# Rotary q of the attention: halves exchanged by row transfers from a copy, sine product on GpSimd, every pair of heads begun three pairs ahead

## The reference, cut to what matters

```
def _rotate_half(x):
    x1, x2 = jnp.split(x, 2, axis=-1)
    return jnp.concatenate([-x2, x1], axis=-1)

def _apply_rope(x, cos, sin):
    return x * cos + _rotate_half(x) * sin
...
q = (x @ Wq).reshape(Bd, Sd, H, DH + D_ROPE)
q_nope, q_rope = (q[..., :DH], q[..., DH:])
c_kv = x @ Wdkv
kv = (c_kv @ Wukv).reshape(Bd, Sd, H, 2 * DH)
k_rope = x @ Wkr
q_rope = _apply_rope(q_rope, cos, sin)
k_rope = _apply_rope(k_rope, cos, sin)
scores = q_nope . k_nope + q_rope . k_rope, scaled and causal
attn = jax.nn.softmax(scores, axis=-1)
```

## Time and profile before

| | us |
|---|---|
| runs of the kernel, median of 3 | 1650.55 |
| the profiled execution | 1647.6 |
| its span (first to last instruction) | 1645.7 |
| attention: first matmul of the stage, last heads | 39.63 to about 443 |

### The profile page before, as it was taken

The page is one execution under the profiler, slowest core; times in us unless marked ns, Lnnn a source line. Parts: engine busy times, 40 slices in busy tenths (PEclk is TensorE's granted clock), DMA queues, the critical chain, the costliest instruction groups (busy, mean ns, idle before and its releaser), DMA issues. The chain is left out here.

```text
span 1645.7 us, 38779 instructions
## 1 busy us (share of the span) xinstructions
PE 1309.8 (80%) x13740; PEld 1003.8 (61%) x13741; DVE 1047.7 (64%) x2173; ACT 611.3 (37%) x1322; POOL 626.1 (38%) x556
## 2 busy tenths in 40 slices
PE   2798999988547999994356878988889539999992
PEld 1355666666436998993223446666667428989981
DVE  6488888978773555554685666666565464555554
ACT  2366676666423333331255721111111213333330
POOL 0254554455203333321003346666666212333320
PEclk9899999999758999997578959999999759999996
DMA  4556566564357111113100000000000257111115
GB/s 139 138 153 175 153 161 188 160 158 145 113 181 303 47 46 51 48 36 121 51 0 13 0 14 2 3 2 3 2 3 2 78 177 287 48 51 45 47 36 166
DMA packets 98815, 145.94 MB, mean 89 GB/s; under 512 B 32961, under 2 KB 76738, under 8 KB 96386
## 3 DMA queue, kind: packets, MB, share of 16 engines
q1 hardware_dynamic: 87746, 118.00, 24.0%
q0 software_dynamic: 8832, 24.13, 4.9%
q10 hardware_dynamic: 2112, 2.10, 0.4%
HBM read 87.57 MB, written 39.32 MB: 77 GB/s over the span
## 5 line engine op out<-in xcount | busy, mean ns | idle before, releaser
L1162 ACT ACTIVATE ffn_h<-ffn_bank,ffn_b 128x256 f32<-128x256 f32 x368 | 154.6, 471 | 323.0 <-PE ffn_bank L114 288.1
L1318 DVE CAST ffn_hh<-ffn_h 128x512 f16<-128x512 f32 x184 | 81.6, 443 | 204.7 <-ACT ffn_h L1162 192.2
L993 POOL DMA_INDIRECT ffn_xs<-xn_rows,ffn_from_rows x92 | 91.4, 994 | 307.5 <-PE ffn_bank L1070 201.3
L2108 POOL TENSOR_TENSOR ssm_GL<-ssm_L,ssml_G 128x512 f32<-128x512 f32 x128 | 165.0, 1298 | 111.5 <-DVE ssm_L L2017 111.4
L112 PE MATMUL ffn_bank<-ffn_hh,ffn_W 128*128 128x256 f16 x736 | 200.6, 273 | 3.8 <-DVE ffn_hl L1320 3.8
L113 PE MATMUL ffn_bank<-ffn_hl,ffn_W 128*128 128x256 f16 x736 | 200.6, 273 | 0.0
L114 PE MATMUL ffn_bank<-ffn_hh,ffn_W 128*128 128x256 f16 x736 | 200.6, 273 | 0.0
L1873 PE MATMUL ssm_Y<-ssm_GL,ssmh_windows 64*32 64x64 f32 x4096 | 148.4, 226 | 7.4 <-POOL ssm_GL L2108 7.0
L2017 DVE TENSOR_TENSOR_SCAN ssm_L<-ssm_bank,ssmh_ident 128x512 f32<-128x512 f32 x128 | 151.5, 1210 | 2.4 <-PE ssm_bank L1856 2.3
L1873 PEld LDWEIGHTS ssm_Y<-ssm_GL,ssmh_windows 64*32 64x32 f32 x4096 | 127.2, 112 | 37.1 <-issue 25.7
L1000 POOL DMA_INDIRECT y_rows<-ffn_y,ffn_to_rows x92 | 90.9, 989 | 143.1 <-DVE ffn_y L1328 129.1
(11 more groups left out here) (339 smaller groups left out, 3254.2 us busy)
## 6 DMA issues: line engine op xcount, KB each, us to landing
ffn_W<-split_w SPq DMA_DIRECT2D x16, 2048.0 KB, 13.6
att_piece<-in_ffn_w SPq DMA_DIRECT2D x32, 512.0 KB, 5.2
split_w<-att_halves SPq DMA_DIRECT2D x32, 512.0 KB, 4.3
att_Q<-att_pair SPq DMA_DIRECT2D x64, 128.0 KB, 2.4
ffn_back<-y_rows SPq DMA_DIRECT2D x16, 512.0 KB, 5.3
att_KB<-att_krl SPq DMA_DIRECT2D x8, 512.0 KB, 5.4
att_Q<-att_pair SPq DMA_DIRECT2D x64, 64.0 KB, 2.0
xn_rows<-ffn_XN SPq DMA_DIRECT2D x8, 512.0 KB, 3.1
```

What stands on the lines that cost most here:

```text
L1162: ins_ = act.activation(h[layer][:, m, :], bank[1 + 2 * layer + u][:, (m % 2) * ST:(m % 2 + 1) * ST], ACT.Gelu, bias=bias[:, ds(e + m, 1)])
L2108: pool.tensor_tensor(GL[:, p % RING, :, :, :].rearrange("p x i n -> p x (i n)"), L[:, p % RING, :, :, :].rearrange("p x i n -> p x (i n)") ...
```

## The change

PE no longer makes the exchanged half from weights of its own: wt, its load, its splitting and the second half of a pair job are gone. ACT copies bank 0 as it is into `turned[:, r % 2, 1, :]` (`high_half`, x = 0). From this copy DVE makes the cosine product, and SP moves the four blocks of 32 rows, exchanged two by two, into a new buffer `swapped` (`swap_rows`, a transfer of its own for each block). POOL multiplies `swapped` by sine, waits for that and adds both products. `job_at` now gives head g the pair g // 2 + 3 where it gave g // 2 + 2, START has a third pair, and SP's `assemble` moves along by one pair. The rotary k keeps its two halves and two products.

```diff
@@ attention_stage
+        swapped = t.sb("swapped", [P, 2, S])
...
-        START = [("qn", 0), ("lat", 0), ("kn", 0), ("kr", 0), ("pair", 0), ("pair", 1), ("v", 0)]
+        START = [("qn", 0), ("lat", 0), ("kn", 0), ("kr", 0), ("pair", 0), ("pair", 1), ("v", 0), ("pair", 2)]
...
             if h % 2 == 0:
-                pr = g // 2 + 2
+                pr = g // 2 + 3
...
+            def swap_rows(pr):
+
+                sp.wait_ge(swap_ready, pr + 1)
+                r = turn["pair", pr]
+                for x in range(4):
+                    rows, others = (slice(y * DR // 2, (y + 1) * DR // 2) for y in (x, x ^ 1))
+                    sp.dma_start(swapped[rows, pr % 2, :], turned[others, r % 2, 1, :]).then_inc(swap_in[pr % 2], 16)
...
             get_nope(("qn", 0), 0)
+            swap_rows(0)
             get_keys(0, 0)
             get_nope(("kn", 0), 0)
+            swap_rows(1)
             assemble(0)
+            swap_rows(2)
             load(0)
             load(1)
             assemble(1)
+            assemble(2)
             for g in range(NG):
                 b, h = divmod(g, NH)
-                if g % 2 == 0 and g >= 2 and g // 2 + 1 < NPR:
-                    assemble(g // 2 + 1)
+                if g % 2 == 0 and g >= 2 and g // 2 + 2 < NPR:
+                    assemble(g // 2 + 2)
+                if g % 2 == 0 and g // 2 + 3 < NPR:
+                    swap_rows(g // 2 + 3)
...
@@ tensor
                 if nth[job]:
                     pe.wait_ge(first_drained, nth[job])
+                    if done[nth[job] - 1][0] == "pair":
+                        pe.wait_ge(swap_ready, done[nth[job] - 1][1] + 1)
...
-                if job is None or job[0] == "lat":
+                if job is None or job[0] in ("lat", "pair"):
                     return
...
-                if what == "pair":
-                    ins = project(bank[1][:, :], wth, wtl, n % (NH // 2) * P, P, n // (NH // 2))
@@ scalar
+                if what == "pair" and x == 0:
+                    r = turn[job]
+                    act.wait_ge(first_ready, nth[job] + 1)
+                    if r >= 2:
+                        act.wait_ge(summed, r - 1)
+                    act.activation(turned[:, r % 2, 1, :], bank[0][:, :], ACT.Copy).then_inc(swap_ready, 1)
+                    return
...
-            for job in START:
+            for job in START[:-1]:
                 high_half(job, 0)
                 high_half(job, 1)
-                high_rope(job)
+            high_rope(("kr", 0))
+            high_rope(("pair", 0))
+            high_half(("pair", 2), 0)
+            high_rope(("pair", 1))
+            high_rope(("pair", 2))
             probs(0, 0)
             probs(0, 1)
@@ vector
-                    if x == 0:
+                    if what == "pair":
+                        dve.wait_ge(swap_ready, n + 1)
+                    elif x == 0:
...
-                        ins = dve.tensor_tensor(to, bank[x][:, :], table[:, :], ALU.mult)
+                        ins = dve.tensor_tensor(to, turned[:, r % 2, 1, :], cosT[:, :], ALU.mult)
@@ gpsimd
+                if what == "pair":
+                    wait_alone(pool, swap_in[n % 2], 64 * (n // 2 + 1), passed)
+                    pool.tensor_tensor(swapped[:, n % 2, :], swapped[:, n % 2, :], sinT[:, :], ALU.mult).then_inc(sin_done, 1)
+                    wait_alone(pool, sin_done, n + 1, passed)
                 wait_alone(pool, first_drained, nth[job] + 1, passed)
...
+                if what == "pair":
+                    pool.tensor_tensor(rope[:, r % 2, :], turned[:, r % 2, 0, :], swapped[:, n % 2, :], ALU.add).then_inc(summed, 1)
+                    return
@@ attention_layer
-        wr, wt, wx = pair("wr", [P, KD, NH * DR]), pair("wt", [P, KD, NH * DR]), pair("wx", [P, KD, NH * DH + LAT + 4 * DR])
+        wr, wx = pair("wr", [P, KD, NH * DR]), pair("wx", [P, KD, NH * DH + LAT + 4 * DR])
```

More of the change, by code:

```diff
@@ L274, in attention_stage @@
 def attention_stage(nc, X, XTh, XTl, weights, identf, identb, upper_neg, cosT, sinT, ffn_w, split_w, nope, xn_rows):
-    (wrh, wrl), (wth, wtl), (wxh, wxl), (wuh, wul), (woh, wol) = weights
+    (wrh, wrl), (wxh, wxl), (wuh, wul), (woh, wol) = weights
     QN_AT, LAT_AT, KR_AT, KT_AT = 0, NH * DH, NH * DH + LAT, NH * DH + LAT + P
@@ L305, in attention_stage @@
         moved = [sem(f"moved{i}") for i in range(2)]
+        swap_ready, swap_in = sem("swap_ready"), [sem(f"swap_in{i}") for i in range(2)]
+        sin_done = sem("sin_done")
         lat_high, qn_high, kn_high, v_high, oT_high = (sem(n) for n in ("lat_high", "qn_high", "kn_high", "v_high", "oT_high"))
@@ L333, in attention_stage @@
         nth = {job: n for n, job in enumerate(done)}
-        nth_second = {job: n for n, job in enumerate(j for j in done if j[0] != "lat")}
+        nth_second = {job: n for n, job in enumerate(j for j in done if j[0] not in ("lat", "pair"))}
         turn = {job: n for n, job in enumerate(j for j in done if j[0] in ("pair", "kr"))}
@@ L517, in second_half @@
                     pe.wait_ge(second_drained, nth_second[job])
-                if what == "pair":
-                    ins = project(bank[1][:, :], wth, wtl, n % (NH // 2) * P, P, n // (NH // 2))
-                elif what == "kr":
+                if what == "kr":
                     ins = project(bank[1][:, :], wxh, wxl, KT_AT, P, n)
@@ L722, in drain @@
                 what, n = job
-                if what == "lat" and x:
+                if what in ("lat", "pair") and x:
                     return
                 if what in ("pair", "kr", "op"):
-                    if x == 0:
+                    if what == "pair":
+                        dve.wait_ge(swap_ready, n + 1)
+                    elif x == 0:
                         dve.wait_ge(first_ready, nth[job] + 1)
@@ L798, in sum_rope @@
                 r = turn[job]
+                if what == "pair":
+                    wait_alone(pool, swap_in[n % 2], 64 * (n // 2 + 1), passed)
+                    pool.tensor_tensor(swapped[:, n % 2, :], swapped[:, n % 2, :], sinT[:, :], ALU.mult).then_inc(sin_done, 1)
+                    wait_alone(pool, sin_done, n + 1, passed)
                 wait_alone(pool, first_drained, nth[job] + 1, passed)
-                wait_alone(pool, second_drained, nth_second[job] + 1, passed)
+                if what == "kr":
+                    wait_alone(pool, second_drained, nth_second[job] + 1, passed)
                 if r >= 2:
                     wait_alone(pool, rope_high, r - 1, passed)
+                if what == "pair":
+                    pool.tensor_tensor(rope[:, r % 2, :], turned[:, r % 2, 0, :], swapped[:, n % 2, :], ALU.add).then_inc(summed, 1)
+                    return
                 pool.tensor_tensor(rope[:, r % 2, :], turned[:, r % 2, 0, :], turned[:, r % 2, 1, :], ALU.add).then_inc(summed, 1)
@@ L2182, in attention_layer @@
         parts = [
-            (rows(ins["att_turned"][0]), *wr), (rows(ins["att_turned"][1]), *wt), (rows(ins["att_mixed"]), *wx),
+            (rows(ins["att_rope"]), *wr), (rows(ins["att_mixed"]), *wx),
             (ins["att_up"], *wu), (rows(ins["L0_attn_a_Wo"]), *wo)]
         layer_norm_stage(nc, "ln0", X, None, XTh, XTl, c["identf"], lambda t: SplitWeights(t, parts))
-        attention_stage(nc, X, XTh, XTl, (wr, wt, wx, wu, wo), c["identf"], identb, upper_neg, cosT, sinT, ffn_w,
+        attention_stage(nc, X, XTh, XTl, (wr, wx, wu, wo), c["identf"], identb, upper_neg, cosT, sinT, ffn_w,
                         split_w, nope, xn_rows)
```

3 lines of the change are left out of this document (1 added, 2 removed).

## The result

The changed kernel took 1675.2 us in the median of 4 runs (1668.46 to 1687.06), the kernel before 1650.0 (1647.85 to 1650.79) beside it: 1.0172 of its time, 95% interval 1.0135 to 1.0208. Forecast were 1667 us, in a range of 1643 to 1692. The runs of the changed kernel also lie wider apart, 19 us against 3; but later the kernel before was run in rounds of 10 to 19 and lay 8 to 11 us apart in each (one slow run of 2065.47 us left out), so four runs say little of that.

What follows compares the result with a forecast made beforehand. A ring of waits through ACT, PE, DVE and POOL, no engine full, was taken as the bound. +3 + 4.3 - 3.7 - 3.3 + 11.5 - 1.6 + 7 = +17.2 us: 1647.6 becomes 1664.8, median about 1667, range 1643 to 1692.

Steps and rivals of the forecast that it cites:

- the beginning: Before the first exponential: ACT's new order delays it from 69.84 to about 81.5, +11.5 us; layer norm saves 1.6.
- the ordinary period: Two heads without an odd job: the new path takes as long as the old, so the period stays at 11.01 us.
- the periods with v: Three periods with rotary k and v: POOL's sine product now stands before the sum, 13.7 us each, +4.3 in all.
- periods with odd jobs, and the rest: Nine periods whose odd job has a second half: one more ACT instruction before the copy, 11.4 instead of 11.10, +3 us.
- Q waits and clock together: Loop: pairs begun earlier end PE's later waits for Q, -3.7 us; four more half-speed stretches cost +7.
- one period of the ring less: End of the loop: last pair begun two heads sooner, one period of 11.01 becomes 7.75 us, -3.3.
- the ring: Attention loop: a circle of waits through ACT, PE, DVE and POOL, no engine full, sets the 11.01 us period.
- queues: periods with op: SP's list: transfers behind the waiting swap_rows come some 1.5 us later but are used a period later; counted 0.
- The relay: ACT's copy, SP's four issues, landing 2.0 us, POOL's two instructions: high part at 16.4, as before.
- The clock: PE's longer waits bring 8 stretches at 1.2 GHz against 4 before, 1.8 us each: +7 us (-7 to +13).
- the rival with the long relay: Row transfers queue behind a load or the keys, or the port delays POOL: about 1693 us; chance 0.17.
- The port: DVE's cosine product and POOL exclude each other at SBUF; within PE's wait, at most 0.6 us a period; counted 0.

Runs made afterwards that it cites:

- a_two_blocks: Changed kernel with only two of the four row transfers for every pair from the third on (q of every second head wrong): 1650.84 us, 1.0021.
- a_start: Changed kernel with ACT's beginning reordered: rotary k's high part behind pair 0's copy, those of pairs 1 and 2 behind the first exponentials: 1670.17 us, 1.0145.
- a_fill: Changed kernel with PE's six second-half matmuls of every pair put back in the loop as work nobody reads: 1679.24 us, 1.0177.
- a_load_behind: Changed kernel with SP's store and load of a weight piece behind the next even head's row transfers instead of ahead: 1677.39 us, 1.0181.
- b_three_ahead: Kernel before, without the exchange, with every pair begun three pairs ahead instead of two: 1644.45 us, 0.9987.
- b_start_late: b_late_high with the high parts of pairs 1 and 2 at the beginning moved behind the first exponentials: 1630.57 us, 0.9902.
- b_late_high: b_three_ahead with ACT making a pair's high part in the next even head, behind its second high_probs: 1634.19 us, 0.9924.
- a_best: Changed kernel with pairs' high parts one head later in the loop, a_start's order at the beginning, and swap_rows ahead of assemble: 1641.95 us, 0.9969.
- a_two_ahead: Changed kernel with every pair begun two pairs ahead again, the exchange by row transfers kept: 1673.45 us, 1.0162.
- a_pieces_behind: a_load_behind with POOL's splitting of a weight piece moved to the odd head, behind the pair's sum and low part: 1674.29 us, 1.0175.

## Why the prediction was right, and which term was missing

The direction was right, the range held, and the beginning, the ordinary period and the periods with v came as forecast: 1675 us where 1667 were forecast. But of the 26.1 us between the two traces 8.4 lie in two terms that the prediction put at nothing. Step by step, from the two profiled executions, first exponential to the last transposition and what lies around:

| term | forecast | measured |
|---|---|---|
| beginning, with the layer norm | +9.9 | +10.6 (80.40 - 69.84), and 1.2 more to the loop's first high part |
| an ordinary period | 11.01 | 11.12 |
| periods with odd jobs, and the rest | +3 | +2.0 |
| periods with v | +4.3 (13.7) | +4.1 (13.58, 13.54, 13.61) |
| Q waits and clock together | +3.3 (-3.7 + 7) | +3.1 |
| one period of the ring less | -3.3 | -3.3 |
| queues: periods with op | 0 | +6.1 |
| behind the attention | 0 | +2.3 |

The measured terms add up to 26.1. The terms of the loop are sums over its periods, each taken above 11.01.

*The relay.* Its length was the riskiest number. It came from SP's L405 and from the rows of POOL, and each piece held: 2.46 for four issues (2.54 forecast), landing 2.0 in the median of 128, the two POOL instructions of 1.27. Only POOL's wait for its own product was 0.37, not the 0.18 of L828, so 0.1 to 0.2 a period. a_two_blocks shows that it is the ring: with two issues less the period of 11.13 fell to 9.86, the other undisturbed ones to no less than 10.2, so the next limit is near. The prediction got the length from its pieces and not by luck; that this length equals that of the old path, so that the ordinary period hardly moved, is a coincidence of this kernel.

*The beginning.* Forecast 79.9 for the first exponential, measured 80.40, and in the series that the prediction named. a_start shows that it was a matter of order: without the exchange touched the last transposition came 8.1 us earlier (447.06 instead of 455.15).

*The clock.* Expected were 8 half-speed stretches against 4. Between 86 and 425 us there are 7, but they are longer: 37 us at half speed in all, against 17. One costs 1.5 to 2.1 us by the rows of a_fill. Those at the changes of sequence only took the place of the ones that the Q waits had brought, so the two terms belong together, as the table has them; the wait before them is now that of v (13.58, then 13.21 at 0.74).

*Queues: the step that failed.* The prediction counted only what SP does behind the waiting `swap_rows`, "0". It should have counted what is ahead of it and in flight. SP in front of the longest period:

```profile
389.90 2.01 SPq L393 DMA_DIRECT2D att_KB<-att_krl  x1
391.95 0.63 SPq L364 DMA_DIRECT2D split_w<-att_halves  x1
392.63 2.32 SPq L359 DMA_DIRECT2D att_piece<-in_ffn_w  x1
395.05 2.17 SPq L411 DMA_DIRECT2D att_Q<-att_pair  x2
397.26 1.27 SPq L416 DMA_DIRECT2D att_Q<-att_pair  x2
398.58 2.50 SPq L401 DMA_DIRECT2D att_swapped<-att_turned  x4
```
```profile
404.35 1.26 POOL L831 TENSOR_TENSOR att_swapped<-att_swapped,attw_sinT 128x512 f32<-128x512 f32 x1 [6.33 <-DMA att_swapped<-att_turned]
```

The copy was ready at 397.10. The transfers were issued 1.5 us late, behind issues that took 2.0 to 2.3 us instead of 0.6, and POOL began 3.27 us behind the last of them instead of 1.58. It happens in the three periods with op, with a DMA share of 0.91 and 0.87 in the two shown, and by another amount in each kernel (the first of the three: 12.52 here, 14.48 in a_fill, 11.92 in a_start). It is the mechanism of the rival with the long relay, in three periods instead of all 28; it may widen the spread of the runs, which nothing here shows. a_load_behind rules out store and load alone; what it is in their place stays open. The 2.3 us behind the attention are not the exchange's: behind the last transposition, where all kernels do the same, the traces took 1214.4 us before, 1216.7 in the changed kernel, 1216.5 in b_three_ahead without the exchange, and between 1210.7 and 1216.4 in b_start_late, b_late_high, a_best, a_start and a_two_ahead.

*The port.* Counted at 0, and right for the changed kernel's ring, but for a reason that I had not seen: POOL stands waiting when the cosine product runs. Where the ring is opened the product runs beside POOL, and DVE, so lengthened, is full.

## What to carry to other kernels

Before saving work on an engine, ask whether that engine or a wait in somebody's list sets the period: here PE was relieved of 1.3 us and DVE of 0.7 in each of 28 periods and nothing came of it, since ACT stood waiting in its list for a chain of hand-overs. Moving a few instructions in ACT's list gave 0.6% by the late high part (0.9924 over 0.9987), and 0.85% with the better beginning (0.9902 over 0.9987), more than any change of the work. A relay over a DMA queue is as long as its issues in a row plus one landing, and whatever is issued or in flight ahead of it is part of its length. When such a ring is opened, look at once for what stood hidden behind it: full engines, the low clock, and instructions of DVE and POOL that exclude each other.

## What the runs showed of the hardware that I had not expected

- SP's issue of one of the 64 KB row transfers took 0.52 to 1.69 us, 0.59 in the median of 128, and single issues of other transfers over 2 us in the period with op shown above (DMA share 0.87).
- POOL waits 0.37 us for its own product (L831 to L839), and 0.18 between the two instructions of a weight piece.
- The half-speed stretches move when work is added or taken away (a_fill, a_load_behind, a_pieces_behind), and a_pieces_behind, whose periods with v were 0.9 to 2.0 us shorter, gained nothing for it. b_start_late, with PE busy for 284.9 of 310 us, has none between 90 and 400 us.
- DVE instructions with both inputs in SBUF took 1.7 and 1.4 times as long in the mean of a_best, where they meet POOL's instructions (1157 against 680, 607 against 426 ns), and those that read PSUM kept their times (546 and 546 ns for the low part of 128x384).
